# Causal attention of the second layer: nine-fold bf16 stacks in one bank each, against plain fp32 on four 32-row tiles of the array

## The chip, the cores and the metric

The kernel runs on one core of one Trainium2 chip. The metric is the device time of one launch in microseconds (us). Three runs of the kernel before took 5902.98, 5903.97 and 5895.77 us, median 5902.98.

## The reference

The program is a two-layer model on x of shape (2, 2048, 128), in fp32. Only the attention of the second layer is touched by the change. Cut to it:

```
x = x + L1_attn(layernorm(x))            # then a mixture-of-experts layer
q, k, v = h @ Wq, h @ Wk, h @ Wv         # 16 heads of 8 columns each
scores  = q k^T / sqrt(8)                # causal: keys up to the query's own position
p       = softmax(scores)                # over up to 2048 keys
out     = (p v) @ Wo                     # per sequence of 2048, 2 sequences
```

Ahead of it stand a retention layer and six layers of windowed attention with feed-forward; behind it the experts. None of these changes.

## The kernel before

Engines are programmed by hand, each with its own instruction stream, and meet only by semaphores. The names below are those of the code.

**Work.** The attention is cut into 8 groups (NG), each of 4 heads (GH) of one sequence. A group is worked in two passes. The first pass finds the largest score of every query: for each of 16 blocks of 128 queries (qt) and each chunk of up to 512 keys (kc) PE multiplies, and DVE takes the maximum over the keys (first_max, line 818). The second pass works with scores turned round (keys on the partitions, 512 queries of a chunk c in the free dimension): an item (c, kt) is one block of 128 keys against one chunk of queries, and a group has 40 items (ITEM). PE makes the scores of 4 heads (second_scores, line 1206), with the negated maximum added through extra rows of the contraction, ACT takes the exponential (exps, line 612), and PE multiplies with the values (second_values, line 1219), whose ninth column of ones sums the probabilities. At the end of a chunk the result is copied, turned and divided by the sum (copy_o, turn_o, store_o).

**Precision.** PE multiplies bf16 here. Each q and each k is written as a sum of three bf16 parts (high, middle, low), and all nine products of parts are stacked on the contraction dimension: 9 x 8 = 72 rows (KR), 75 with the three parts of the maximum. The parts are made once for all heads after the projection (lines 1174 to 1177 on PE, 596 to 601 on ACT, 804 and 808 on DVE), written to a buffer in DRAM (line 347) and read back for each group as stacks (load_stacks, lines 355 and 359) into RA with TOK, or RB with XC. The causal mask on a diagonal block is one more bf16 product that is added (tri_q in line 1194, tri_k in line 1209). The values are multiplied in plain fp32, the four heads in four column tiles of the array (9 columns each at 0, 32, 64, 96).

**Order.** att_step(g) does the first pass of group g between the items of the second pass of group g - 1. Per item PE runs: scores of heads 0 and 1 into the pair of banks D01, scores of heads 2 and 3 into D67, half of the item's four first-pass products (one head each, in turn into the two banks of D23), the values of the item before, the other half. So there are nine steps: a first one with the first pass alone, seven mixed ones (the middle six in a hardware loop), and a last one with the second pass alone. A step begins when the stacks of its group have arrived (stacks_in0, stacks_in1); they are loaded into the buffers that the group two before has left, after its last product. At the end of a step DVE combines the maxima, splits them in three parts (split_max), PE turns them, and SP copies them as rows into the stack (max_rows, line 367).

## Time and profile before

| | us |
|---|---|
| median of three runs | 5902.98 |
| the profiled execution | 5908.11 |
| its span, first to last instruction | 5906.1 |
| second-layer attention within the span, from its first projection (3911.5) to the first product of its output projection (5268.5) | 1357 |

| engine | busy us | share of the span |
|---|---|---|
| PE matmul | 5179.1 | 88% |
| PE weight load | 3133.2 | 53% |
| DVE | 3948.9 | 67% |
| ACT | 2684.4 | 45% |
| POOL | 2643.7 | 45% |

The mean granted clock of TensorE is 0.916 of full speed. Shares over the whole span say little here, since the attention in question is 23% of it and has its own pace. Matmuls are pipelined, and the duration of one in the trace holds the time in which its results drain; how close two of them follow each other is read from their starts. An fp32 matmul stands in the trace as two records, each with its own weight load.

### The profile page before, as it was taken

The page shows a single profiled execution, that of the slowest core. Times are in us where ns is not written, and L with a number is a line of the kernel's source. Part 1 is how long each engine was busy: PE and PEld are TensorE (multiplying, and loading weights), DVE is VectorE, ACT ScalarE, POOL GpSimd, SP SyncE. Part 2 cuts the span into 40 slices and gives each one's busy share as a digit, 9 for nine tenths or more (in the row PEclk, how much of TensorE's full clock was granted, in tenths as well). Part 3 has the DMA queues.
Part 4 walks back from the last instruction along what each step waited for, and adds up shares of the span by engine and source line. Part 5 has one row for each costly group of instructions (what it writes and reads, how often), then busy time and mean ns, then how long its engine had stood idle before and what let it go on. Part 6 is the DMA issues. An engine that isn't in the chain of part 4 may idle for free.

```text
span 5906.1 us, 163733 instructions
## 1 busy us (share of the span) xinstructions
PE 5179.1 (88%) x71504; PEld 3133.2 (53%) x71696; DVE 3948.9 (67%) x5079; ACT 2684.4 (45%) x3457; POOL 2643.7 (45%) x947
## 2 busy tenths in 40 slices
PE   8899889988998899989998899867777887798999
PEld 5566556664666466646665566532222222246776
DVE  5988488956986588748983889437566666623333
ACT  1565445644665365535653556421444444451111
POOL 2888378845885488628881788310000000000000
PEclk7999899989999899989998999875888888888999
DMA  1111101110111011101111111020111000100000
GB/s 51 31 37 37 46 27 37 39 53 19 39 37 60 12 38 37 39 34 35 37 39 40 31 37 39 20 62 14 17 18 17 12 12 12 17 33 2 4 4 5
DMA packets 94224, 173.85 MB, mean 29 GB/s; under 512 B 23641, under 2 KB 35554, under 8 KB 91874
## 3 DMA queue, kind: packets, MB, share of 16 engines
q1 hardware_dynamic: 93538, 163.67, 10.6%
q8 instruction: 557, 9.13, 0.7%
q14 instruction: 129, 1.06, 0.1%
HBM read 55.71 MB, written 8.39 MB: 11 GB/s over the span
## 4 chain that ended last, share of the span: by engine, by line
PE 76%; DVE 8%; issue 5%; ACT 4%; DMA 3%; POOL 2%; SPq 1%; DVEq 0%; ACTq 0%; POOLq 0%
PE D L1127 7%; PE D L1046 6%; PE D L1061 5%; PE D L1068 5%; PE D L1191 4%; PE D L978 4%; PE D L1219 4%; PE D L1310 4%; PE D L1085 4%; PE D L1026 3%; PE D L1206 3%; PE D L1094 3%; PE D L1096 3%; PE D L1034 3%; DVE mxp L818 3%
## 5 line engine op out<-in xcount | busy, mean ns | idle before, releaser
L423 POOL TENSOR_TENSOR rn<-ss,mhalf 128x32 f32<-128x32 f32 x192 | 1212.2, 6313 | 314.3 <-DVE ss L711 312.2
L818 DVE TENSOR_REDUCE mxp<-D 128x1 f32<-128x512 f32 (+3 forms) x1280 | 722.2, 606 | 417.6 <-PE D L1194 268.9
L612 ACT ACTIVATE hh<-D 128x1024 f32<-128x1024 f32 (+1 forms) x320 | 283.8, 936 | 605.5 <-PE D L1209 477.0
L1127 PE MATMUL D<-PTb,V 64*64 64x32 f32 x24576 | 415.7, 222 | 60.2 <-issue 42.8
L769 DVE TENSOR_TENSOR TOK<-D,RA 128x1024 f32<-128x1024 f32 x384 | 466.4, 1215 | 0.0
L428 POOL TENSOR_TENSOR hh<-hh,rr 128x1024 f32<-128x1024 f32 x192 | 364.6, 1899 | 219.8 <-DVE rr L739 219.5
L432 POOL TENSOR_TENSOR XC<-XC,TOK 128x1024 f32<-128x1024 f32 x132 | 311.5, 2360 | 335.2 <-DVE TOK L769 335.0
L1127 PEld LDWEIGHTS D<-PTb,V 64*64 64x64 f32 x24576 | 396.7, 138 | 102.5 <-issue 102.1
L709 DVE TENSOR_REDUCE ss<-TOK 128x32 f32<-128x2048 f32 x192 | 436.9, 2276 | 1.1 <-POOL rn L423 1.1
L558 ACT ACTIVATE V<-D 128x512 f32<-128x512 f32 x384 | 229.3, 597 | 451.5 <-PE D L1094 384.7
L263 POOL TENSOR_TENSOR rstd<-var_s,mhalf 128x4 f32<-128x4 f32 x96 | 96.3, 1007 | 717.2 <-DVE var_s L238 717.2
L1046 PE MATMUL D<-OTb,RB 128*128 128x128 f32 x3072 | 396.5, 285 | 14.7 <-ACT OTb L515 13.6
L1061 PE MATMUL D<-RB,XN 128*128 128x512 f32 x768 | 372.9, 609 | 40.3 <-DVE TOK L769 39.4
L1046 PEld LDWEIGHTS D<-OTb,RB 128*128 128x128 f32 x3072 | 378.9, 201 | 17.6 <-ACT OTb L515 15.1
L765 DVE TENSOR_TENSOR XC<-D,RA 128x1024 f32<-128x1024 f32 x264 | 321.6, 1218 | 90.2 <-ACT TOK L547 82.8
L1068 PE MATMUL D<-RB,XN 128*128 128x512 f32 x768 | 365.5, 599 | 2.6 <-DVE TOK L769 2.4
L515 ACT ACTIVATE OTb<-D 128x1024 f32<-128x1024 f32 x192 | 196.9, 1025 | 321.8 <-PE D L1127 321.8
L547 ACT ACTIVATE TOK<-D 128x1024 f32<-128x1024 f32 x192 | 196.4, 1023 | 304.1 <-PE D L1061 218.8
L612 ACT ACTIVATE V<-D 128x1024 f32<-128x1024 f32 (+2 forms) x320 | 256.3, 851 | 166.9 <-PE D L1206 88.0
L434 POOL TENSOR_TENSOR XC<-XC,TOK 128x1024 f32<-128x1024 f32 x132 | 311.6, 2361 | 0.0
L1085 PEld LDWEIGHTS D<-kTb,qTb 64*32 64x32 f32 x24576 | 254.0, 105 | 89.0 <-issue 89.0
L1191 PE MATMUL D<-TOK,RA 72*128 72x512 bf16 (+3 forms) x640 | 229.9, 407 | 80.1 <-DMA TOK<-parts_dram 44.9
(219 smaller groups left out, 10307.2 us busy)
## 6 DMA issues: line engine op xcount, KB each, us to landing
V<-V SPq DMA_DIRECT2D x936, 64.0 KB, 2.0
V<-V SPq DMA_DIRECT2D x192, 192.0 KB, 2.4
RA<-tabs_dram SPq DMA_DIRECT2D x6, 2048.0 KB, 7.8
RB<-watt_dram SPq DMA_DIRECT2D x6, 2048.0 KB, 12.2
parts_dram<-hh SPq DMA_DIRECT2D x48, 128.0 KB, 2.3
RA<-parts_dram SPq DMA_DIRECT2D x12, 384.0 KB
TOK<-parts_dram SPq DMA_DIRECT2D x36, 128.0 KB
RB<-parts_dram SPq DMA_DIRECT2D x12, 384.0 KB
```

The lines of the kernel that those rows point to most:

```text
L423: pool.tensor_tensor(rn[:, st % 2, :], ss[:, :], mhalf[:, :], ALU.pow).then_inc(s["powed"], 1)
L428: pool.tensor_tensor(sh, sh, rr[:, :].unsqueeze(2).to_broadcast([P, HEADS, 64]), ALU.mult).then_inc(s["pnorm"], 1)
L612: act.activation(PTE[n % 2][:, 2 * half:2 * half + 2, 0:CH - r * P], ST2[half][:, :, 0:CH - r * P], ACT.Exp, scale=float(HD) ** -0.5)\
L709: dve.tensor_reduce(ss[:, :], SQH.rearrange("p (a d) -> p a d", d=DH), AX.X, ALU.add).then_inc(s["reduced"], 1)
L769: return dve.tensor_tensor(swapped.rearrange("p (a q d) -> p a q d", q=2, d=32), src[:, :].rearrange("p (a q d) -> p a q d", q=2, d=32)[:, ...
L818: dve.tensor_reduce(mxp[:, h, qt, kc:kc + 1], PB[2 + n % 2][:, 0:first_pass_keys(qt, kc)], AX.X, ALU.max).then_inc(s["max1"], 1)
L1046: m = pe.matmul(D23[:, 0:P], WO[:, p, :], OTb[:, n % 2, p * P:(p + 1) * P], start=(p == 0), stop=(p == PAIRS - 1))
L1061: m = pe.matmul(PB[x], xb, WQ[:, x * CH:(x + 1) * CH], start=True, stop=True)
L1068: m = pe.matmul(PB[2 + x], xb, WK[:, x * CH:(x + 1) * CH], start=True, stop=True)
L1085: m = pe.matmul(D45[32 * r:32 * r + 32, at:at + 64], qTb[hs, p * P + 32 * r:p * P + 32 * r + 32], KT[n % 2][hs, p, 32 * r:32 * r + 64], st ...
L1127: m = pe.matmul(D01[64 * h:64 * h + 64, at:at + WIN], VW[n % 2][ks, (0 if r % 2 else 2) + h, p * DH:(p + 1) * DH], PTb[ks, p * P + 32 * r: ...
L1191: m = pe.matmul(bank[:, 0:keys], QST[p][0:KR, h * SEQ + qt * P:h * SEQ + (qt + 1) * P], KST[p][0:KR, h * SEQ + kc * CH:h * SEQ + kc * CH + ...
```

## The change

The stacks in bf16 and their way through DRAM go. The projection of q and k (project_group, line 1150 of the changed kernel) is made per group in fp32 with weights that are laid out so that each of the 4 heads has its 8 rows at the start of its own 32 partitions (wqk); one full product gives one chunk of q or k, 8 per group, and ACT copies it to SBUF (copy_qk). In the k copy a bias of one fills the ninth row of every head, and SP writes the negated maxima into the ninth row of q (max_rows), so that a second-pass product contracts 9 rows and a first-pass product 8. The four heads sit in four 32-row tiles of the array. A product of one head is one fp32 matmul of 128 stationary columns.

The work is cut into units of two heads (hp = 0 or 1): S units (second-pass scores) and F units (first pass). A unit takes one of three pairs of banks, D01, D23 and D67, in turn (pair_of), and waits for the reader of the unit three places ahead of it (released_by). One flat sequence of 320 items replaces the steps: at place `at` PE runs S0 and S1 of item at - 20 (LAG), F0 and F1 of first-pass item `at`, and the values of item at - 21. ACT takes the exponential of a unit at a time, DVE the maxima of two heads in one instruction. The mask of the first pass is still the added tri_q; that of the second pass is now a POOL instruction on the probabilities (cut_diagonal). Maxima are combined, turned and written per chunk, not per group. DVE's copy of the result goes to ACT (copy_o). Everything is written out, with no hardware loop.

```diff
+        WQK = OTb[:, 0, :].rearrange("p (a g n) -> p a g n", a=2, g=4)
+        QK = [[r[:, 0:SEQ], r[:, SEQ:2 * SEQ]] for r in (RA[:, :], RB[:, :], XS)]
...
+        PTE = [hh[:, 0:4, :], V2[:, :, :], V3[:, :, :]]
...
+        PAIR = [D01, D23, D67]
...
-        FIRST = [(h, qt, kc) for h in range(GH) for qt in range(NT) for kc in range(qt // 4 + 1)]
-        NF = len(FIRST) // ITEMS
-        assert NF * ITEMS == len(FIRST)
+        FIRST = [(qt, kc) for qt in range(NT) for kc in range(qt // 4 + 1)]
+        assert len(FIRST) == ITEMS
+        TOTAL = NG * ITEMS
+        LAG = 20
+        ENDS = [4, 12, 24, 40]
...
+        def units_at(at):
+            return [(kind, at, hp) for kind, hp in (("S", 0), ("S", 1), ("F", 0), ("F", 1))
+                    if (at >= LAG if kind == "S" else at < TOTAL)]
+        UNITS = [u for at in range(TOTAL + LAG) for u in units_at(at)]
+        UNIT_NO = {u: m for m, u in enumerate(UNITS)}
+        def pair_of(unit):
+            return PAIR[UNIT_NO[unit] % 3]
+        def released_by(unit):
+            m = UNIT_NO[unit] - 3
+            if m < 0:
+                return None, 0
+            kind, at, hp = UNITS[m]
+            return ("exp2", 2 * (at - LAG) + hp + 1) if kind == "S" else ("max1", 2 * at + 1 + hp)
...
+        def proj_at(at):
+            g, n = divmod(at, ITEMS)
+            x, rest = divmod(n - 4, 4)
+            return (g + 1, x // 2, x % 2) if g + 1 < NG and rest == 0 and 0 <= x < 8 else None
...
+            def max_rows(cg):
+                g, c = divmod(cg, CB)
+                sp.wait_ge(s["neg_copied"], cg + 1)
+                for h in range(GH):
+                    sp.dma_start(QK[g % 3][0][32 * h + HD:32 * h + HD + 1, c * CH:(c + 1) * CH].rearrange("r (x n) -> r x n", n=P),
+                                 nT[4 * h:4 * h + 4, cg % 2, :]).then_inc(s[f"neg_rows{cg % 2}"], 16)
...
+                pool.affine_select(out=PTE[i % 3][:, :, 0:P], in_=PTE[i % 3][:, :, 0:P], compare_op=ALU.is_ge, fill=0.0, base=0,
+                                   pattern=[[0, GH], [1, P]], channel_multiplier=-1).then_inc(s["diag_cut"], 1)
...
+            def copy_qk(g, c, qk):
+                act.wait_ge(s["qk_proj"], g * 8 + 2 * c + qk + 1)
+                dst = QK[g % 3][qk][:, c * CH:(c + 1) * CH]
+                if qk == 0:
+                    act.activation(dst, PB[5], ACT.Copy).then_inc(s["qk_copied"], 1)
+                else:
+                    act.activation(dst, PB[5], ACT.Identity, bias=ones_row).then_inc(s["qk_copied"], 1)
+            def exps(i):
+                g, n = divmod(i, ITEMS)
+                c, kt = ITEM[n]
+                r = max(0, kt - 4 * c)
+                if i >= 3:
+                    act.wait_ge(s["pv2"], i - 2)
+                for hp in range(2):
+                    act.wait_ge(s["score2"], 2 * i + hp + 1)
+                    act.activation(PTE[i % 3][:, 2 * hp:2 * hp + 2, 0:CH - r * P],
+                                   pair_of(("S", i + LAG, hp))[:, :].rearrange("p (h n) -> p h n", h=2)[:, :, 0:CH - r * P],
+                                   ACT.Exp, scale=float(HD) ** -0.5).then_inc(s["exp2"], 1)
...
-                dve.tensor_reduce(mxp[:, h, qt, kc:kc + 1], PB[2 + n % 2][:, 0:first_pass_keys(qt, kc)],
-                                  AX.X, ALU.max).then_inc(s["max1"], 1)
...
+                dve.tensor_reduce(mxp[:, 2 * hp:2 * hp + 2, qt, kc],
+                                  pair_of(("F", at, hp))[:, :].rearrange("p (h n) -> p h n", h=2)[:, :, 0:keys], AX.X, ALU.max)\
+                   .then_inc(s["max1"], 1)
...
+            def project_group(g, c, qk):
+                hg, b = divmod(g, 2)
+                if misc["qk_copied"]:
+                    misc_free()
+                pe.matmul(PB[5], WQK[:, qk, hg, :], chunk(XC, b * CB + c), start=True, stop=True).then_inc(s["qk_proj"], 1)
+                misc["qk_copied"] += 1
+            def first_pass(at, hp):
+                g, n = divmod(at, ITEMS)
+                qt, kc = FIRST[n]
                 keys = first_pass_keys(qt, kc)
-                if not (isinstance(g, int) and g == 0 and n < 2):
-                    pe.wait_ge(s["max1"], g * len(FIRST) + n - 1)
                 diag = kc == qt // 4
-                bank = PB[2 + n % 2]
-                m = pe.matmul(bank[:, 0:keys], QST[p][0:KR, h * SEQ + qt * P:h * SEQ + (qt + 1) * P],
-                              KST[p][0:KR, h * SEQ + kc * CH:h * SEQ + kc * CH + keys], start=True, stop=not diag)
+                if hp == 0 and qt % 4 == 0 and kc == 0:
+                    pe.wait_ge(s["qk_copied"], 8 * g + 2 * (qt // 4) + 2)
+                sem_name, count = released_by(("F", at, hp))
+                if count:
+                    pe.wait_ge(s[sem_name], count)
+                banks = pair_of(("F", at, hp))
+                for x in range(2):
+                    rows = slice(32 * (2 * hp + x), 32 * (2 * hp + x) + HD)
+                    m = pe.matmul(banks[:, x * CH:x * CH + keys], QK[g % 3][0][rows, qt * P:(qt + 1) * P],
+                                  QK[g % 3][1][rows, kc * CH:kc * CH + keys], start=True, stop=not diag)
                 if diag:
-                    m = pe.matmul(bank[:, keys - P:keys], ident_b[:, :], tri_q[:, :], start=False, stop=True)
+                    for x in range(2):
+                        m = pe.matmul(banks[:, x * CH + keys - P:x * CH + keys], ident_b[:, :], tri_q[:, :], start=False, stop=True)
                 m.then_inc(s["score1"], 1)
-            def second_scores(g, p, n):
+            def second_scores(i, hp):
+                g, n = divmod(i, ITEMS)
                 c, kt = ITEM[n]
                 r = max(0, kt - 4 * c)
-                for half in range(2):
-                    it = g * ITEMS + n
-                    pe.wait_ge(s["exp2"], 2 * it + half + 1)
-                    for x in range(2):
-                        h = 2 * half + x
-                        q0 = h * SEQ + c * CH + r * P
-                        m = pe.matmul(ST2[half][:, x, 0:CH - r * P], KST[p][0:KR + 3, h * SEQ + kt * P:h * SEQ + (kt + 1) * P],
-                                      QST[p][0:KR + 3, q0:q0 + CH - r * P], start=True, stop=kt < 4 * c)
-                        if kt >= 4 * c:
-                            m = pe.matmul(ST2[half][:, x, 0:P], ident_b[:, :], tri_k[:, :], start=False, stop=True)
-                    m.then_inc(s["score2"], 1)
...
+                pe.wait_ge(s["exp2"], 2 * i + 2)
+                if kt >= 4 * c:
+                    pe.wait_ge(s["diag_cut"], diagonals(i))
...
+            def turn_max(cg):
+                misc_free()
+                pe.wait_ge(s["max_all"], cg + 1)
+                pe.transpose(PB[5][0:GH * CB, 0:P], mxa[:, :, :].rearrange("p h x -> p (h x)"), ident).then_inc(s["neg_turned"], 1)
+                misc["neg_copied"] += 1
...
-                for n in range(ITEMS):
-                    if g2:
-                        second_scores(g - 1, p2, n)
-                    if g1:
-                        for x in range(NF // 2):
-                            first_pass(g, p1, n * NF + x)
...
+            for at in range(TOTAL + LAG + 4):
+                i = at - LAG
+                if 0 <= i < TOTAL:
+                    second_scores(i, 0)
+                    second_scores(i, 1)
+                if at < TOTAL:
+                    first_pass(at, 0)
+                    first_pass(at, 1)
+                if 1 <= i <= TOTAL:
+                    second_values(i - 1)
+                if chunk_end(at - 2) is not None:
+                    turn_max(chunk_end(at - 2))
+                if chunk_end(i - 3) is not None:
+                    turn_o(chunk_end(i - 3))
+                if proj_at(at) is not None:
+                    project_group(*proj_at(at))
...
+    wqk = np.zeros((128, 2, 4, 4, 32), np.float32)
+    for x, n in enumerate("qk"):
+        wqk[:, x, :, :, 0:8] = a["L1_attn_W" + n].T.reshape(128, 4, 4, 8)
+    d["wqk"] = wqk.reshape(128, 2, 4, 128)
```

PE, one full item in a step of before: S units of an item are L1206 (D01, D67), first-pass products L1191 (D23), the mask L1194, values L1219.

```order
L1206 MATMUL D01<-RA,TOK 128x512 [waits exp2]
L1206 MATMUL D01<-RA,TOK 128x512
L1202 REGISTER_ALU
L1206 MATMUL D67<-RA,TOK 128x512 [waits exp2]
L1206 MATMUL D67<-RA,TOK 128x512
L1188 REGISTER_ALU
L1191 MATMUL D23<-XC,RB 128x512 [waits max1]
L1188 REGISTER_ALU
L1191 MATMUL D23<-XC,RB 128x512 [waits max1]
L1219 MATMUL D45<-V2,qTb 9x512 [waits exp2]
L1219 MATMUL D45<-V2,qTb 9x512 x3
```

PE, the same place in the changed kernel: L1187 are the S units, L1167 the F units, L1171 the mask, L1204 the values; this is one full item and the scores of the next.

```order
L1187 MATMUL D01<-RA 128x512 [waits exp2]
L1187 MATMUL D01<-RA 128x512
L1187 MATMUL D23<-RA 128x512 [waits max1]
L1187 MATMUL D23<-RA 128x512
L1167 MATMUL D67<-RB 128x512 [waits max1]
L1167 MATMUL D67<-RB 128x512
L1167 MATMUL D01<-RB 128x512 [waits exp2]
L1167 MATMUL D01<-RB 128x512
L1204 MATMUL D45<-V2,qTb 9x512 [waits exp2]
L1204 MATMUL D45<-V2,qTb 9x512 x3
```

Where S had D01 and D67 to itself and F the two banks of D23, all three pairs now go round: the second F unit takes over the pair D01 from the first S unit of the same item, and stands ahead of the values.

PE, an item of the changed kernel whose F units lie on the diagonal, and at which a chunk's maxima are turned (L1212):

```order
L1167 MATMUL D01<-RB 128x256 [waits max1]
L1167 MATMUL D01<-RB 128x256
L1171 MATMUL D01<-tri_q,ident_b 128x128 x2
L1167 MATMUL D23<-RB 128x256 [waits exp2]
L1167 MATMUL D23<-RB 128x256
L1171 MATMUL D23<-tri_q,ident_b 128x128 x2
L1204 MATMUL D45<-V3,qTb 9x512 [waits diag_cut,exp2]
L1204 MATMUL D45<-V3,qTb 9x512 x3
L1212 MATMUL D45<-con,mxa 16x128 [waits o_stored,max_all,neg_copied,qk_copied]
```

The mask product follows each F unit, between products in row tiles, and the values wait for POOL's cut too. Chunk work that stood at the end of a step now stands between items.

## Rows read from the trace of the kernel before

**Rows 1.** Busy time by stretch: start:end, length, then each engine, PEclk, DMA share, GB/s

```profile
3911.00:3988.00 77.00, 25.41 (x100) 15.57 (x100) 21.52 (x35) 22.47 (x41) 16.05 (x12) 0.68 0.57 121
3988.00:4104.00 116.00, 87.42 (x227) 19.93 (x226) 93.10 (x172) 0.00 (x0) 0.00 (x0) 0.50 0.10 16
4104.00:4231.00 127.00, 118.00 (x785) 42.84 (x783) 97.42 (x196) 67.53 (x80) 1.00 (x4) 0.96 0.00 1
4231.00:4262.00 31.00, 0.00 (x0) 0.00 (x0) 0.00 (x0) 0.00 (x0) 0.00 (x0) 0.50 0.54 78
5179.00:5269.00 90.00, 82.07 (x570) 23.27 (x571) 5.73 (x24) 68.42 (x82) 0.00 (x0) 0.93 0.04 9
```

**Rows 2.** One line each: duration ns min/median/max, first and last start

```profile
L1174 PE MATMUL D<-XC,wC x16: 592/595/1219, 3911.5 to 3940.3; 128*128 128x512 f32 x16
L966 PE MATMUL D<-TOK,wC x16: 592/594/697, 5268.5 to 5277.7; 128*128 128x512 f32 x16
```

**Rows 3.** SP's queue in order of time: start, us, engine, line, count

```profile
4099.63 1.79 SPq L367 DMA_DIRECT2D RA<-nT  x3
...
4231.00 1.75 SPq L367 DMA_DIRECT2D RB<-nT  x3
...
4233.57 1.03 SPq L359 DMA_DIRECT2D TOK<-parts_dram  x3
...
5178.67 1.75 SPq L367 DMA_DIRECT2D RB<-nT  x3
```

**Rows 4.** Timeline of two full items within a mixed step

```profile
4347.55 1.94 ACT L612 ACTIVATE V<-D 128x1024 f32<-128x1024 f32 x2 [1.67 <-PE D L1206]
...
4350.36 1.94 ACT L612 ACTIVATE hh<-D 128x1024 f32<-128x1024 f32 x2 [0.87 <-PE D L1206]
```

**Rows 5.** Narrow windows of the timeline at one item's values, last step

```profile
5256.11 0.38 PE L1206 MATMUL D<-RB,XC 75*128 75x512 bf16 x1
...
5256.42 0.62 PE L1219 MATMUL D<-hh,PTb 128*9 128x512 f32 x4
...
5256.85 0.61 PE L1219 MATMUL D<-hh,PTb 128*9 128x512 f32 x4
5257.39 0.10 PEld L1206 LDWEIGHTS D<-RB,XC 75*128 75x128 bf16 x1 [0.86 <-ACT V L612]
```

**Rows 6.** Timeline, last step: what releases PE and what releases ACT

```profile
5253.89 1.94 ACT L612 ACTIVATE hh<-D 128x1024 f32<-128x1024 f32 x2 [0.26 <-PE D L1206]
...
5255.88 0.11 PEld L1206 LDWEIGHTS D<-RB,XC 75*128 75x128 bf16 x2 [0.57 <-ACT hh L612]
...
5257.90 0.22 PE L1209 MATMUL D<-tri_k,ident_b 128*128 128x128 bf16 x1
...
5258.16 1.02 ACT L612 ACTIVATE hh<-D 128x1024 f32<-128x1024 f32 x1 [0.38 <-PE D L1209]
```

**Rows 7.** Timeline of fp32 products in the layers ahead: full array, then tiles

```profile
3004.73 0.33 PE L1026 MATMUL D<-con,SQ 128*128 128x128 f32 x1
...
3004.73 1.09 PE L1026 MATMUL D<-con,SQ 128*128 128x128 f32 x8
...
3000.68 1.94 PE L1127 MATMUL D<-PTb,V 64*64 64x32 f32 x116
...
3012.28 0.26 PE L1085 MATMUL D<-kTb,qTb 64*32 64x64 f32 x4
```

**Rows 8.** Groups by line and form: busy us, mean ns, idle before

```profile
L612 ACT ACTIVATE hh<-D 128x1024 f32<-128x1024 f32 x256 | 248.8, 1021 | 556.7 <-PE D L1209 428.2 <-PE D L1206 128.4
L612 ACT ACTIVATE hh<-D 128x512 f32<-128x512 f32 x64 | 34.9, 595 | 48.8 <-PE D L1209 48.8
...
L755 DVE TENSOR_REDUCE mx<-D 128x16 f32<-128x1024 f32 x192 | 232.8, 1212 | 6.9 <-PE D L1085 6.5
```

**Rows 9.** One line: duration ns min/median/max, start

```profile
L446 POOL TENSOR_SCALAR_AFFINE_SELECT tri_q<-tri_q x1: 292/292/292, 3910.0 to 3910.0; 128x128 bf16<-128x128 bf16 x1
```

**Rows 10.** The page's DMA issues: count, KB each, us to landing

```profile
parts_dram<-hh SPq DMA_DIRECT2D x48, 128.0 KB, 2.3
```

More of the change, by code:

```diff
@@ L382, in _ @@
+            for cg in range(CHUNKS):
+                max_rows(cg)
+            sp.wait_ge(s["pv2"], TOTAL)
             sp.dma_start(EW1, t["ew1"].rearrange("e p n -> p e n")).then_inc(s["moew_in"], 16)
@@ L591, in _, with copy_o @@
+            def copy_o(cg):
+                g, c = divmod(cg, CB)
+                act.wait_ge(s["pv2"], g * ITEMS + ENDS[c])
+                if cg >= 1:
+                    act.wait_ge(s["o_turned"], cg)
+                act.activation(oTs, PB[4], ACT.Copy).then_inc(s["o_copied"], 1)
+            for c in range(CB):
+                for qk in range(2):
+                    copy_qk(0, c, qk)
             for c in range(NC):
                 act.wait_ge(s["c_proj"], c + 1)
-                if c >= 2:
-                    act.wait_ge(s[f"split_out{c % 2}"], 96 * (c // 2))
@@ L897, in _ @@
+            for at in range(TOTAL + LAG + 4):
+                if at < TOTAL:
+                    first_max(at, 0)
+                    first_max(at, 1)
+                if chunk_end(at) is not None:
+                    chunk_max(chunk_end(at))
+                if chunk_end(at - 2) is not None:
+                    negate_max(chunk_end(at - 2))
+                if chunk_end(at - LAG - 3) is not None:
+                    store_o(chunk_end(at - LAG - 3))
             for c in range(NC):
@@ L1212, in second_values @@
-            def second_values(g, p, n):
+                if hp == 0 and kt == 0:
+                    cg = g * CB + c
+                    pe.wait_ge(s[f"neg_rows{cg % 2}"], 64 * (cg // 2 + 1))
+                sem_name, count = released_by(("S", i + LAG, hp))
+                pe.wait_ge(s[sem_name], count)
+                banks = pair_of(("S", i + LAG, hp))
+                for x in range(2):
+                    rows = slice(32 * (2 * hp + x), 32 * (2 * hp + x) + HD + 1)
+                    m = pe.matmul(banks[:, x * CH:x * CH + CH - r * P], QK[g % 3][1][rows, kt * P:(kt + 1) * P],
+                                  QK[g % 3][0][rows, c * CH + r * P:(c + 1) * CH], start=True, stop=True)
@@ new lines, in _ @@
+            for c in range(NC):
+                if c >= 2:
+                    pe.wait_ge(s["c_vcopy"], c - 1)
+                for b in range(NBLK):
+                    m = pe.matmul(PB[6 + c % 2][:, b * P:(b + 1) * P], XC[:, c * CH + b * P:c * CH + (b + 1) * P], wC[:, 0, :],
+                                  start=True, stop=True)
+                m.then_inc(s["c_proj"], 1)
+            pe.wait_ge(s["tri_ready"], 2)
+            pe.wait_ge(s["o_zero"], 1)
+            pe.wait_ge(s["c_vcopy"], NC)
```

349 lines of the change are left out of this document (103 added, 246 removed).

## The prediction

> **What bounds the kernel now.** I read the busy time by stretch first. Within the span the attention runs from its first projection at 3911.5 us to the first output projection at 5268.5 us [rows 2], 1357 us, and only this part changes. The stretches [rows 1] show four phases. For 77 us bf16 parts are made, stored and loaded again (PE busy 25 us). Then 116 us of first pass alone, at PEclk 0.50. Mixed steps of 127 us follow at 0.96, with PE busy for 118 and DVE for 97; between two of them stand 31 us with no engine at work, while DMA is at 0.54. A last stretch of 90 us has no first pass. SP's queue tells why the 31 us are there: the maxima's rows of a group leave at 4231.00, and the next stacks are asked for only behind them, from 4233 on [rows 3]. From 4099.6 to 5178.7 there are 7 steps, 154 us each on average.
>
> Within a step the timeline has ACT begin two full items at 4347.55 and 4350.36, 2.81 us apart, with ACT idle for 0.87 of them [rows 4]. PE fills this: four bf16 score products, four first-pass products and the values. ACT's pair takes 1.94 us, so PE's order of work is the pace, and DVE is second.
>
> **What goes.** The parts, their way through DRAM and 7 x 31 = 217 us of empty array between steps; also about 10 us at half clock behind each of these (a step has 0.96). A product of scores drops from 72 or 75 rows of bf16 to 8 or 9 of fp32. An fp32 product of 512 columns makes two records 0.43 us apart [rows 5], so it streams for 0.853 us, four times a bf16 one; if four row tiles work at once, the four heads cost 0.853 us as before. So the multiplying itself gains nothing, and the question is how items follow each other.
>
> **Do tiles overlap?** The values are four products in four column tiles; four first records stand at 5256.42 and four second ones at 5256.85 [rows 5], so all four run at once. For row tiles the nearest rows are tiles of 64 rows: 116 records of 64x64 tiles lie in 1.94 us, at most 17 ns each [rows 7], so a set of eight takes at most 0.134 us, while two loads of 64 columns in one tile need 0.109 (a 128-column load has a pitch of (1.09 - 0.33)/7 = 0.109 us). Four such tiles, two up and two across, work nearly together. The set is at most 0.025 us longer than one tile alone, at most 0.05 for loads of 128 columns. I take full overlap, with 0.03 us per unit for loads that meet. The bounds: 0, and 0.21 if the loads of the two heads queue (two loads of 0.109 ahead of the second head).
>
> **The new chain.** In the order S0, S1, F0, F1, values, with three pairs of banks, unit m waits for the reader of unit m - 3. F1 of an item thus waits until ACT has read S0 of the same item, and the values stand behind F1 on PE. The next S0 stands behind the values. With w for the us that a product streams (0.853 for 512 columns):
> - S0 from start to ACT: load 0.057 (a first record of 128 columns takes 0.33, of which it streams for 0.107 and drains for 0.165, [rows 7]), w, drain 0.165 (0.592 of L966 less 0.427, [rows 2]), release 0.04 (the mask ends at 5258.12, ACT starts at 5258.16, [rows 6]).
> - ACT: 0.595 for 512 and 1.021 for 1024 elements [rows 8], so w + 0.167; PE starts 0.05 behind its end (5253.89 + 1.94 = 5255.83, load at 5255.88, [rows 6]).
> - F1: 0.057 + w, no drain in the way.
> - Values: 0.01 + w, and a change of tiles on either side: 0.10 before (the bf16 product streams until 5256.11 + 0.21 = 5256.32, next load 5256.42) and 0.10 behind (stream ends 5257.28, load 5257.39) [rows 5].
>
> A full item: 4 x 0.853 + 0.262 + 0.167 + 0.05 + 0.057 + 0.01 + 0.19 = 4.15 us, against 2.81 now. In this time ACT works for 1.94 and DVE for 2 x 1.21 (128x1024 maxima, L755, [rows 8]); neither is the bound, and PE itself stands idle only from F0's end (1.8) to F1's start (2.2).
>
> A group has 17408 columns a head in 40 items, 85% of full, so 4 w are 2.90. Fixed parts 0.74, loads that meet 0.06. In 16 of 40 items F lies on the diagonal: the two mask products need the whole array, 0.26 us on F1 and some 0.05 a mean item where F0's mask delays F1 (narrow S beside a wide F). That is 0.16 a mean item. Sum 3.85 us, or 154 a group.
>
> **Work between items.** Eight projections a group, each 0.853 + 0.057 + one more change of tiles 0.10 = 1.01. They write a bank of their own and ACT's copy (0.6) lies beside the next S0. 52 of them: 52 us. Turning the maxima, 32 x 0.25, and the result, 32 x 0.59 (four at the pitch of 0.109 and a change): 27 us, of which the second was there before. POOL's cut of 512 elements is at most 4 x 0.29 = 1.2 us [rows 9] and has 3 us until the values ask for it: nothing; without this cover it would be 16 x 1.2 a group. The rows of maxima need four issues at 0.6 (three took 1.79, [rows 3]) and, like the parts, 2.3 us to land [rows 10]; with the turning and the negation some 5.2 us, and the tightest chunk has two items, 6.6 us: nothing, but close.
>
> **Ends.** Before the sequence: 8 projections, each followed by its copy since they share a bank, 1.75 us at full clock and more at half, and the values' projection: 27 us. Then 20 places with F alone. There DVE is the pace, 2.4 us for the two maxima of a full item [rows 8]; these places have 79% of the full columns, so 38 us, and 50 with masks, first latency and four projections at half clock. At the end 20 items without F, 2.0 each: 40 us, and 5 to the output projection. When S joins, some 8 us pass at the half clock.
>
> Sum: 27 + 50 + 300 x 3.85 + 52 + 27 + 40 + 5 + 8 = 1364 us, against 1357. The profiled execution took 5908.11, of which 5906.1 is span; 7 more is 5915, and the median of the runs lies 5 lower than that execution: 5910 us. Within 0.2%, about 12 us, a measurement cannot tell it from no change, so what the 217 us of empty steps give back the longer items take.
>
> **The rivals.**
> (B) Row tiles overlap only in part. For it: no row of the trace has tiles of 32 rows by 128 columns. Against: the 17 ns [rows 7]. The price: loads that queue, 0.21 on S and 0.21 on F1 in place of 0.06, 0.36 x 300 = 108, and up to 0.2 w more for the streams; 5990 to 6090, say 6030. It is decided on PE between the first and last record of four score products. The Trainium skill (TensorE: Matmul & The Clock Gate, Part 3, Measured speedup) states 3.07 times for four row tiles at N=512. By it a set would take 1.30 streams, 0.22 more on S and as much on F1, 0.44 x 300 = 130 us; no run here shows it yet.
> (C) The clock falls. For it: the first pass alone ran at 0.50 for 116 us with PE 75% busy in the records [rows 1], and the array is now idle or half filled in part of each item. Against: the last step, with its own waits, keeps 0.93. At 1.2 GHz three of the four streams double (ACT's stays): 3 x 0.725 and the masks, +2.3 us an item; half of the 300 items so cost 340 us, 6250, all of them 6600.
> (D) Row tiles run one after another: eight streams an item, +3 us, about 6800. The four records in one window of 0.04 us of L1085, in 64-row tiles, [rows 7] speak against it.
> (E) Faster: changes of tiles and loads hide (loads run ahead of products wherever no wait stands before them), 0.19 + 0.11 off each item: 300 x 0.30 = 90, 5820. Against: each change of tiles in rows 5 costs its 0.10.
>
> **How the numbers follow.** The forecast, chain and overlap as worked out, has 48%; its own range is 5870 to 5955, since 0.13 us an item is 40 us, and it falls 18 faster, 10 within 0.2%, 20 slower. B 20%, C 15%, D 4%, E 13%. That makes 31% faster, 10% the same, 59% slower. The range 5835 to 6270 holds the forecast, B and half of C, and leaves out D, the upper half of C and half of E, together under 20%.
>
> **What would show it.** Right, if full items in the middle follow at 4.1 to 4.2 us on ACT, with ACT idle for 2.2 of them; if L1167's second unit starts 0.05 us behind the end of the first exponential of its item, and L1204 right behind it; if four first records of L1187 stand within 0.1 us; if no stretch of 30 us without work is left; if PEclk is 1.0 in the mixed part. B shows in the starts of L1187's records, C in PEclk. Wrong in another way: if PE mostly waits for max1, DVE is in the chain, and I have left it out; if it waits for neg_rows or diag_cut, a cover named above was too thin.

## The result and the profile after

| | us |
|---|---|
| median after, 4 runs | 6738.0 (6723.49 to 6742.88) |
| median before, 4 runs beside them | 5899.38 (5891.22 to 5903.97) |
| ratio, 95% interval | 1.1419 [1.1396, 1.1442] |
| profiled span after | 6721.8 |
| granted clock over the span | 0.805, before 0.916 |

The change costs 839 us. The forecast was 5910, the range 5835 to 6270: wrong in sign and in size.

First the place. The output projection's first product, and the group projections (duration ns, then first and last start):

```profile
L932 PE MATMUL D<-TOK,wC x16: 592/595/1219, 6084.1 to 6094.6; 128*128 128x512 f32 x16
L1150 PE MATMUL D<-XC,OTb x128: 637/1114/1223, 3892.0 to 5709.5; 128*128 128x512 f32 x128
```

From 3892.0 to 6084.1 are 2192 us, against 1357 in [rows 2], 835 more. (This execution reached the attention 19.5 us earlier than the one before, 3892.0 against 3911.5, so the two spans differ by 816; behind the attention both take 638.) The whole loss lies in the attention. A projection product here has a median of 1114 ns; those of the output projection, the same shape, have 595. Something slows TensorE in this stage and lets go of it behind it. The profile's clock line (40 slices, tenths of full speed) and the stretches, with the columns of [rows 1], say what:

```profile
PEclk8999899899989998998999855555555555557999
```

```profile
3911.00:3945.00 34.00, 32.23 (x156) 17.57 (x155) 12.25 (x16) 6.66 (x11) 1.32 (x6) 0.65 0.00 1
3945.00:4000.00 55.00, 54.99 (x184) 19.09 (x182) 31.24 (x33) 8.23 (x11) 2.21 (x6) 0.50 0.00 0
4000.00:4100.00 100.00, 99.57 (x377) 29.54 (x379) 33.85 (x36) 26.50 (x34) 3.81 (x6) 0.50 0.00 1
5000.00:5100.00 100.00, 98.60 (x401) 29.18 (x397) 33.35 (x34) 27.01 (x35) 6.02 (x12) 0.55 0.00 1
6000.00:6050.00 50.00, 50.00 (x209) 11.80 (x205) 10.31 (x10) 18.02 (x22) 2.54 (x4) 0.50 0.00 1
```

Read them against [rows 1]. The 31 us without work are gone, and so is the DMA (share 0.54, now 0.00). But where a mixed step was granted 0.96, the stage now gets 0.50 to 0.55 from 3945 to 6050: nearly always the lower of the two levels, 1.2 GHz. It does so with PE at work for 98.60 of 100 us, so PE is not short of work. The Trainium skill (TensorE: Matmul & The Clock Gate, Part 1) lets the clock fall when the engine has been idle; these rows do not agree with that as the cause.

Now one full item. ACT's exponentials, four items in a row, then one item on all engines, then a narrow window (5007.095 to 5007.14) at its first products (timeline: start, us, engine, line; x is the count of records):

```profile
4912.02 1.94 ACT L608 ACTIVATE V<-D 128x1024 f32<-128x1024 f32 x2 [5.41 <-PE D L1187]
4919.12 1.94 ACT L608 ACTIVATE V<-D 128x1024 f32<-128x1024 f32 x2 [5.16 <-PE D L1187]
4926.21 1.94 ACT L608 ACTIVATE hh<-D 128x1024 f32<-128x1024 f32 x2 [5.16 <-PE D L1187]
4933.30 1.94 ACT L608 ACTIVATE V<-D 128x1024 f32<-128x1024 f32 x2 [5.16 <-PE D L1187]
```

```profile
5007.10 2.09 PE L1187 MATMUL D<-RA 9*128 9x512 f32 x8
5008.12 0.34 PEld L1167 LDWEIGHTS D<-RB 8*128 8x128 f32 x2 [0.50 <-issue]
...
5009.29 1.94 ACT L608 ACTIVATE hh<-D 128x1024 f32<-128x1024 f32 x2 [4.49 <-PE D L1187]
5010.36 0.50 PEld L1167 LDWEIGHTS D<-RB 8*128 8x128 f32 x4 [1.05 <-ACT hh L608]
...
5012.37 1.90 PE L1204 MATMUL D<-V,PTb 128*9 128x512 f32 x8
...
5014.20 0.52 PEld L1187 LDWEIGHTS D<-RA 9*128 9x128 f32 x8 [1.70 <-issue]
```

```profile
5007.10 0.30 PEld L1187 LDWEIGHTS D<-RA 9*128 9x128 f32 x4 [1.70 <-issue]
5007.10 1.24 PE L1187 MATMUL D<-RA 9*128 9x512 f32 x4
```

and the same line in this item, with the durations of its eight records (ns min/median/max; an fp32 product has two records, so four heads have eight):

```profile
L1187 PE MATMUL D<-RA x8: 1056/1136/1218, 5007.1 to 5008.1; 9*128 9x512 f32 x8
```

Three things stand here. The four first records together last 1.24 us, and the longest one of the eight 1.218: they start within 0.02 us, so the row tiles do run together. All eight records of four heads span 2.09 us with their drain. One after another four heads would stream for 4 x 2 x 0.853 = 6.8 us at this clock; here they take less than a third of it. By the 3.07 times that the Trainium skill states for four row tiles (TensorE: Matmul & The Clock Gate, Part 3, Measured speedup), and that the prediction cited under rival B, they would take an estimated 2.2 us before any drain, so this trace has more overlap than that.

The order of events is the predicted chain: S, first exponential, F1 0.05 behind its end (5009.29 + 1.02 = 5010.31, load at 5010.36), values, next S. And every leg on PE (the time from one event of the chain to the next) has about twice its forecast length: S to ACT 2.19, F1 to values 2.01, values to the next S 1.83; with ACT's 1.07 the item is 7.10, and ACT's rows stand 7.09 to 7.10 apart. The forecast was 4.15.

### The profile page after: what moved, and what is told of

Read it like the earlier page. It is cut to its first block, busy times and chain, and to the rows that moved or that the text cites. A ratio compares the mean times of both kernels' runs of the same rounds, so it can differ in the third digit from the quotient of the medians.

```text
span 6721.8 us, 164570 instructions
## 1 busy us (share of the span) xinstructions
PE 6315.2 (94%) x73664; PEld 3422.5 (51%) x73856; DVE 3857.7 (57%) x4247; ACT 2723.0 (41%) x3521; POOL 2710.1 (40%) x1071
## 4 chain that ended last, share of the span: by engine, by line
PE 86%; DVE 4%; ACT 4%; issue 3%; POOL 2%; DMA 0%; DVEq 0%; SPq 0%; ACTq 0%; POOLq 0%
PE D L1167 13%; PE D L1187 8%; PE D L1204 7%; PE D L1093 6%; PE D L1012 5%; PE D L1027 4%; PE D L1034 4%; PE D L944 4%; PE D L1294 4%; PE D L1051 3%; PE D L992 3%; PE D L1060 3%; PE D L1000 3%; PE D L1062 3%; PE D L1125 2%
## 5 line engine op out<-in xcount | busy, mean ns | idle before, releaser
L820 DVE TENSOR_REDUCE mxp<-D 128x2 f32<-128x1024 f32 (+3 forms) x640 | 677.8, 1065 | 1342.9 <-PE D L1167 812.0
L608 ACT ACTIVATE V<-D 128x1024 f32<-128x1024 f32 (+3 forms) x426 | 359.1, 894 | 842.8 <-PE D L1187 841.9
L463 POOL TENSOR_SCALAR_AFFINE_SELECT V<-V 128x512 f32<-128x512 f32 x84 | 53.3, 634 | 1260.1 <-ACT V L608 1260.1
L429 POOL TENSOR_TENSOR XC<-XC,TOK 128x1024 f32<-128x1024 f32 x132 | 311.6, 2361 | 334.9 <-DVE TOK L781 334.7
L1167 PE MATMUL D<-RB 8*128 8x512 f32 (+2 forms) x960 | 359.9, 935 | 9.1 <-ACT V L608 8.0
L1167 PE MATMUL D<-RA 8*128 8x512 f32 (+2 forms) x960 | 354.8, 950 | 7.2 <-ACT V L608 4.0
L608 ACT ACTIVATE hh<-D 128x1024 f32<-128x1024 f32 (+1 forms) x214 | 179.3, 889 | 434.5 <-PE D L1187 434.3
L463 POOL TENSOR_SCALAR_AFFINE_SELECT hh<-hh 128x512 f32<-128x512 f32 x44 | 27.9, 634 | 808.2 <-ACT hh L608 808.2
```

Source lines behind the costliest of these rows:

```text
L608: act.activation(PTE[i % 3][:, 2 * hp:2 * hp + 2, 0:CH - r * P], pair_of(("S", i + LAG, hp))[:, :].rearrange("p (h n) -> p h n", h=2)[:, : ...
L820: dve.tensor_reduce(mxp[:, 2 * hp:2 * hp + 2, qt, kc], pair_of(("F", at, hp))[:, :].rearrange("p (h n) -> p h n", h=2)[:, :, 0:keys], AX.X ...
L1167: m = pe.matmul(banks[:, x * CH:x * CH + keys], QK[g % 3][0][rows, qt * P:(qt + 1) * P], QK[g % 3][1][rows, kc * CH:kc * CH + keys], start ...
```

## The experiments

Theory 1: the clock is granted low because few rows of the array take part in the products (8 or 9 of each 32). Theory 2: it is low because of waits and changes between units. S is a second-pass unit, F a first-pass unit, 0 and 1 are the pairs of heads (hp). The kernel before, run beside each of them, had medians from 5899.7 to 5907.1; where two runs lie close, their ratios compare them better than their medians. The clock is the mean over the whole span.

| run | what differs from the changed kernel | median us | ratio to before, 95% | granted clock |
|---|---|---|---|---|
| e1_rows32 | 32 rows in F and S | 5948.81 | 1.0080 [1.0063, 1.0097] | 0.948 |
| e10_rows24 | 24 rows | 5983.03 | 1.0125 [1.0094, 1.0155] | 0.939 |
| e6_rows16 | 16 rows | 6710.2 | 1.1358 [1.1327, 1.1388] | 0.811 |
| e8_first_pass_rows32 | 32 rows in F, 9 in S | 6641.7 | 1.1239 [1.1206, 1.1273] | 0.824 |
| e2_values_early | values between F0 and F1 | 6900.3 | 1.1692 [1.1669, 1.1715] | 0.789 |
| e3_alternating | order S0, F0, S1, F1 | 6892.75 | 1.1679 [1.1656, 1.1702] | 0.795 |
| e4_rows32_values_early | 32 rows, values between | 6048.49 | 1.0227 [1.0201, 1.0254] | 0.928 |
| e5_rows32_alternating | 32 rows, order S0, F0, S1, F1 | 5982.31 | 1.0128 [1.0108, 1.0149] | 0.948 |
| e7_rows32_no_mask1 | 32 rows, no first-pass mask | 5899.8 | 0.9982 [0.9970, 0.9994] | 0.949 |
| e12_crossed_no_mask1 | e7, units crossed | 5898.84 | 0.9996 [0.9984, 1.0008] | 0.948 |
| e9_before_few_rows | kernel before, 8 and 11 rows | 6686.83 | 1.1318 [1.1286, 1.1351] | 0.802 |
| e11_before_no_mask1 | kernel before, no first-pass mask | 5890.0 | 0.9974 [0.9960, 0.9987] | 0.917 |

**All 32 rows.**

```diff
-                    rows = slice(32 * (2 * hp + x), 32 * (2 * hp + x) + HD)
+                    rows = slice(32 * (2 * hp + x), 32 * (2 * hp + x) + 32)
...
-                    rows = slice(32 * (2 * hp + x), 32 * (2 * hp + x) + HD + 1)
+                    rows = slice(32 * (2 * hp + x), 32 * (2 * hp + x) + 32)
```

> Every product of scores, in both passes, contracts all 32 rows of its tile in place of 8 or 9; the added rows hold zeros, so order, streams, loads and results stay as in the changed kernel. Theory 1 (the clock falls because the products fill too few rows of the array): the granted clock is about 1.0 through the mixed part and the time falls to where the chain was forecast, 5880 to 5960 us. Theory 2 (the clock falls because PE has gaps in every item, while it waits for the first exponential and between changes of tiles): rows change nothing, clock 0.5 to 0.55, 6738 us within 0.3%.

Two slices, and 789 us come back (6738.0 to 5948.8). Number of instructions, columns, waits and order are those of the changed kernel, and the added rows add nothing: they are zeros on both sides, but for the ninth row of k in F, which holds ones against zeros in q. The profile's clock line and two stretches of this run, the second one long:

```profile
PEclk8999899989998999989998999879999999998999
```

```profile
5000.00:5100.00 100.00, 94.02 (x621) 30.30 (x621) 55.76 (x56) 43.01 (x56) 8.60 (x16) 1.00 0.00 1
...
3990.00:5200.00 1210.00, 1129.04 (x7528) 369.81 (x7522) 635.85 (x684) 522.29 (x648) 80.56 (x144) 1.00 0.00 1
```

The clock is 1.00 over 1210 us, and PE is busy for less of the time than it was at half clock (94.02 against 98.60 of 100). Theory 1 holds, at 5948.8 within its 5880 to 5960, and this run also shows what the kernel would have been on the forecast's assumption. The same four legs, at the full clock:

```profile
4916.94 1.94 ACT L608 ACTIVATE hh<-D 128x1024 f32<-128x1024 f32 x2 [2.41 <-PE D L1187]
...
4918.02 0.30 PEld L1167 LDWEIGHTS D<-TOK 32*128 32x128 f32 x4 [1.15 <-ACT hh L608]
...
4919.08 1.05 PE L1204 MATMUL D<-V,PTb 128*9 128x512 f32 x8
...
4920.05 0.31 PEld L1187 LDWEIGHTS D<-TOK 32*128 32x128 f32 x8 [0.86 <-issue]
4920.06 1.14 PE L1187 MATMUL D<-TOK 32*128 32x512 f32 x8
```

```profile
4921.29 1.94 ACT L608 ACTIVATE V<-D 128x1024 f32<-128x1024 f32 x2 [2.41 <-PE D L1187]
```

```profile
L1187 PE MATMUL D<-TOK x8: 587/640/692, 4920.1 to 4920.6; 32*128 32x512 f32 x8
```

From ACT to ACT 4.35 us: 1.08 + 1.06 + 0.98 + 1.23. The forecast had 1.07, 1.01, 0.96 and 1.115. Of S's records, in the last fence, the longest (a first one, behind its load) has 0.692 and the shortest 0.587, so 0.105 of load stands bare, not 0.057. The same 0.105 fits F1's leg (0.105 + 0.853 + 0.10 = 1.06). S's records end at 4921.20 (4920.06 + 1.14) and ACT starts at 4921.29, a release of 0.09 where the forecast had 0.04. Of the excess of 0.19, the load twice makes 0.10 and the release 0.05; 0.04 is spread over the rest.

**The dose.** In the same two slices, 16 and then 24 rows; and 32 rows in the first pass's slice alone.

> 16 of the 32 rows of each row tile take part (the added rows are zeros), in place of 8 or 9 in the changed kernel and 32 in e1_rows32. Instructions, streams and loads are the same. Theory 1 (the share of rows that take part decides the granted clock) expects a granted clock between the two, and a time between them: 6100 to 6500 us if the clock follows the rows smoothly; 5940 to 5960 or 6720 to 6750 if it has a step on one side of 16 rows. Theory 2 (the gaps between units decide, and e1_rows32 only filled something else) expects no order by rows at all.

> 24 of the 32 rows of each row tile take part (the added rows are zeros). e6_rows16 ran at 6710 us, e1_rows32 at 5949. Theory 1 expects a time between them; 6000 to 6500 us if the clock follows the rows, 5945 to 5960 or 6690 to 6720 if it has one step.

> 32 rows take part in the first pass's products alone; those of the second pass keep their 9 rows (the changed kernel has 8 and 9, e1_rows32 has 32 and 32). Theory 1 in the form that each stream counts by its own rows expects a time between the two, 5950 to 6500 us, with a granted clock between 0.80 and 0.95; in the form that it takes the whole item above some share, it expects either 5945 to 5960 (above it) or 6730 to 6745 (below it).

One hundred us of each, sixteen rows, then twenty-four (two stretches), then the first pass alone (two stretches):

```profile
5000.00:5100.00 100.00, 98.71 (x384) 28.87 (x382) 30.35 (x32) 28.31 (x34) 3.18 (x5) 0.53 0.00 1
```

```profile
4500.00:4600.00 100.00, 95.94 (x531) 30.92 (x531) 47.33 (x49) 36.75 (x50) 8.55 (x16) 0.81 0.00 1
5000.00:5100.00 100.00, 93.82 (x622) 30.51 (x624) 54.00 (x56) 42.55 (x56) 8.56 (x16) 1.00 0.00 1
```

```profile
4500.00:4600.00 100.00, 99.57 (x379) 30.19 (x375) 33.05 (x36) 26.07 (x34) 3.81 (x6) 0.50 0.00 1
5000.00:5100.00 100.00, 98.38 (x450) 31.00 (x447) 38.61 (x40) 28.81 (x40) 8.56 (x16) 0.62 0.00 1
```

It is no even slope: 16 rows give back 28 us of the 789, little more than the runs of one kernel differ by, and 24 rows give back 755. With 24 the clock is full in some stretches and not in others. Neither time lies in a range that was expected: 6710.2 stands 10 us under the step's 6720 to 6750, and 5983.0 between the step's 5945 to 5960 and the slope's 6000 to 6500. Filling F alone gives back 96 us, far less than half; with S at its 9 rows the clock stays low most of the time. The expectation for e8 in its first form (5950 to 6500) was missed by 142 us, though its clock of 0.824 lies in the 0.80 to 0.95, and so was the second, since a part does come back.

**The converse, in the kernel before.**

```diff
-                m = pe.matmul(bank[:, 0:keys], QST[p][0:KR, h * SEQ + qt * P:h * SEQ + (qt + 1) * P],
-                              KST[p][0:KR, h * SEQ + kc * CH:h * SEQ + kc * CH + keys], start=True, stop=not diag)
+                m = pe.matmul(bank[:, 0:keys], QST[p][64:KR, h * SEQ + qt * P:h * SEQ + (qt + 1) * P],
+                              KST[p][64:KR, h * SEQ + kc * CH:h * SEQ + kc * CH + keys], start=True, stop=not diag)
```

> The converse, in the kernel before: its score products contract rows 64 to 72 and 64 to 75 alone, 8 and 11 rows of bf16 in place of 72 and 75; so 64 rows of parts are left out of the scores. Columns, instructions and waits stay. Theory 1 expects that the granted clock of the mixed steps falls from 0.96 towards 0.5 and the time rises by several hundred us (mixed steps of 127 us have 118 us of PE, so up to 100 us more in each of 8 groups: 6300 to 6700 us). The rival, that the fall needs fp32 streams in row tiles and not few rows in themselves, expects 5890 to 5930 us.

(The second pass's rows, KR + 3, begin at 64 in the same way. The 64 rows left out hold parts of q and k, so this run's scores are wrong and only its time is of use.) Groups, 4700 to 4800 us (line, shapes, count | busy us, mean ns), and a long stretch of this run:

```profile
L1206 PE MATMUL D<-RA,TOK 11*128 11x512 bf16 x60 | 28.9, 623 | 0.0
L1191 PE MATMUL D<-XC,RB 8*128 8x512 bf16 x52 | 28.4, 617 | 0.0
```

```profile
3990.00:5200.00 1210.00, 1046.69 (x3531) 245.98 (x3531) 511.68 (x994) 290.22 (x337) 4.03 (x16) 0.50 0.07 10
```

The same loss, in bf16, without row tiles, with DMA between the steps: 780 us slower than its kernel before, clock 0.50 over 1210 us. Fewer rows in each score product, with columns, instructions and waits as they were, took the clock away. So fp32 scores, row tiles, the grouping and the new waits are not needed for the loss. The rows left out held data, so this run alone would not tell the number of rows from what is in them; e1_rows32 does, since it adds zeros.

**The gaps.** The values moved between F0 and F1, and the alternating order, at 8 and 9 rows.

```diff
                 if at < TOTAL:
                     first_pass(at, 0)
-                    first_pass(at, 1)
                 if 1 <= i <= TOTAL:
                     second_values(i - 1)
+                if at < TOTAL:
+                    first_pass(at, 1)
```

```diff
-                if 0 <= i < TOTAL:
-                    second_scores(i, 0)
-                    second_scores(i, 1)
-                if at < TOTAL:
-                    first_pass(at, 0)
-                    first_pass(at, 1)
+                for hp in range(2):
+                    if 0 <= i < TOTAL:
+                        second_scores(i, hp)
+                    if at < TOTAL:
+                        first_pass(at, hp)
```

(In the second, the list that numbers the units is changed alike.)

> The values of the item before stand between the two first-pass units, so PE has work while the first exponential runs. Theory 2 (gaps): the clock goes up for most of the mixed part, and with a full item of about 3.9 us the time is 5850 to 6100. Theory 1 (rows): the clock stays at 0.5 to 0.55; PE is then full in each item (S 1.87, F 1.7 + 1.87, values 1.7, changes of tiles 0.4: 7.5 us against 7.1 now), and the time is 6700 to 6880 us.

> Units alternate S0, F0, S1, F1 on PE and in the turn of the three pairs, in place of S0, S1, F0, F1. At either theory the chain is nearly the same, since F1 still takes over the pair of S0 and stands ahead of the values; F0 stands between S0 and S1, so that only two tiles work at the start of an item. Theory 1: clock 0.5 to 0.6, 6700 to 6900 us. Theory 2: the gap before F1 becomes smaller (S1 and F0 fill it), so the clock may rise in part of the stretch: 6100 to 6600 us.

The stretch from 5000 to 5100 us, first of e2_values_early, then of e3_alternating:

```profile
5000.00:5100.00 100.00, 99.69 (x382) 28.79 (x374) 28.39 (x34) 26.67 (x31) 2.54 (x4) 0.50 0.00 1
```

```profile
5000.00:5100.00 100.00, 100.00 (x356) 32.13 (x355) 26.99 (x32) 25.82 (x29) 2.54 (x4) 0.52 0.00 1
```

PE is at work for all or nearly all of the time, and the clock is as low as ever (0.50, 0.52). Both orders cost some 160 us more; e2_values_early lies 20 us above the 6700 to 6880 that theory 1 gave it. Theory 2 falls as the cause of this loss.

**The same two orders at 32 rows.**

> All 32 rows of each row tile take part (the added rows are zeros, as in e1_rows32), and the units of an item alternate again: S0, F0, S1, F1, with the values last. It asks what the grouping itself is worth at the full clock. Theory 1 (the granted clock falls because few rows of the array take part) expects a granted clock near that of e1_rows32 (0.95) and a time between 5900 and 6020 us: in this order S1 waits for nothing but its own bank, F1 waits for the reader of S0, and a chain counted as for the grouped order comes to about the same 4.35 us for a full item. At the half clock alternating had cost 155 us more than grouping; theory 3 (grouping is worth the same 155 us at either clock, since it keeps the two S units' products and their loads in a row) expects 6080 to 6120 us.

> All 32 rows take part as in e1_rows32, and the values of the item before stand between F0 and F1 instead of behind F1, so that PE does not idle while it waits for the first exponential. If the prediction's chain is the bound as it was told (the wait of F1 for the exponential of S0), filling that wait takes up to 0.4 us off a full item: 5830 to 5880 us. The rival is that three pairs of banks for four units bind in any order: F1 then ends later, DVE's maximum of it (1.21 us) holds F0 of the next item, and the chain F1, drain 0.165, maximum 1.21, F0, values comes to 4.4 us: 5950 to 6010 us.

Grouping against alternating is worth 34 us at the full clock (5982.3 - 5948.8) and 155 at the half clock (6892.8 - 6738.0). So that part of the change is a gain at either level, and not the loss. Putting the values early is 100 us slower, 6048.5 where even the rival had 5950 to 6010; the waits (us in total, times, longest, from 5000 to 5100) and a stretch, first of e1_rows32, then of e4_rows32_values_early:

```profile
PEld D L1167 <- DVE mxp L820: 3.0, 9, 0.8
```

```profile
PEld D L1167 <- DVE mxp L820: 13.7, 19, 1.3
```

```profile
4100.00:4200.00 100.00, 95.95 (x569) 30.43 (x566) 45.60 (x50) 39.30 (x50) 7.28 (x14) 0.88 0.00 1
```

The wait for DVE's maximum (3.0 to 13.7 us of the 100) takes in part the place of the one for the exponential (19.8 to 12.0), as the rival said; but the clock is also below full in part of the run (0.88 here), so how the 100 us divide between the two stays open. It also says that 32 rows alone do not secure the full clock: here the order took some of it away, and no run shows why.

**The mask products.** In the first pass they are left out, so the maximum is taken over the future keys of the diagonal block too, another shift of the same exponentials; once on e1_rows32, once on the kernel before.

```diff
-                if diag:
-                    for x in range(2):
-                        m = pe.matmul(banks[:, x * CH + keys - P:x * CH + keys], ident_b[:, :], tri_q[:, :], start=False, stop=True)
```

> As e1_rows32, and the mask products of the first pass are left out: the maximum of a row is then taken over the future keys of the diagonal block too, which is another shift of the same exponentials. In e1_rows32 the two mask products stood in 16 of 40 items at 0.26 us. If PE is the chain there (theory 1, the prediction's chain), they cost 300 x 0.4 x 0.26 = 31 us and some 10 more from F0's mask and the places with F alone: 5905 to 5925 us, against 5949 for e1_rows32. The rival, that ACT's and DVE's readers set the pace of the diagonal items and the masks lie beside them, expects 5940 to 5955 us.

> The kernel before without the mask products of its first pass, as e7_rows32_no_mask1 has it (5900 us, 50 below e1_rows32). It asks whether that gain belongs to the row tiles. The kernel before has 16 mask products of 128 columns in bf16 a head and group, 0.06 us each as a stream: 64 x 8 x 0.06 = 31 us if PE is its pace everywhere, 5870 to 5885 us. The rival, that the first pass's reader on DVE (one maximum a head) sets the pace of those products, expects 5895 to 5907 us.

49 us off with row tiles by the medians (24 to 44 expected), 58 by the ratios; 17 off the kernel before, between the 22 to 37 of the one theory and the up to 12 of the other. With row tiles the mask stands in the chain. From e1_rows32, F1, its mask and the values of one item:

```profile
5263.75 1.13 PE L1167 MATMUL D<-RB 32*128 32x512 f32 x4
...
5264.81 0.28 PE L1171 MATMUL D<-tri_q,ident_b 128*128 128x128 bf16 x2
...
5265.02 1.05 PE L1204 MATMUL D<-V,PTb 128*9 128x512 f32 x8
```

The values start 1.27 us behind F1 in place of the 1.06 above, so the mask costs 0.21; in 16 of 40 items of 300 that is 25 us, about half of the gain, and the rest is not placed. With the mask gone the kernel of row tiles is level with the kernel before (0.9982), and so is the kernel before without its mask (0.9974): the two intervals overlap. So the row tiles gain nothing here over an old kernel that is given the same saving.

**Crossed units.** S of heads 0, 1 with F of heads 2, 3, and then the other way round, on top of e7: in the alternating order above, F's rows and the place of its maximum take `1 - hp` for `hp`.

> Built on e7_rows32_no_mask1 (32 rows, no mask products in the first pass; 5899.8 us). The units of an item alternate, but crossed: S of heads 0 and 1 with F of heads 2 and 3, then S of heads 2 and 3 with F of heads 0 and 1, then the values. Neighbouring units stand in other row tiles and have other readers (ACT and DVE), so each pair of streams may overlap: three streams in an item in place of four, and the second exponential no longer waits behind the first. If streams on PE are the bound, an item loses up to 0.6 us: 5750 to 5850 us. If three pairs of banks for four units are (a unit holds its pair for 0.107 + 0.853 + 0.165 + 0.04 and its reader, 1.02 or 1.21, and one stream of the values with its changes stands between), the order changes little: F of heads 0 and 1 still waits for the exponential and the next F for the other one, 5885 to 5910 us. The alternating order of e5_rows32_alternating lost 33 us; if its loss came from the same cause, this one loses it too: 5920 to 5945 us.

```profile
4916.38 0.70 PE L1184 MATMUL D<-TOK 32*128 32x512 f32 x2
4916.39 0.19 PEld L1167 LDWEIGHTS D<-RA 32*128 32x128 f32 x2
4916.40 0.70 PE L1167 MATMUL D<-RA 32*128 32x512 f32 x2
...
4917.36 1.02 PE L1184 MATMUL D<-TOK 32*128 32x512 f32 x4
...
4917.62 1.94 ACT L608 ACTIVATE hh<-D 128x1024 f32<-128x1024 f32 x2 [1.98 <-PE D L1184]
4918.69 0.30 PEld L1167 LDWEIGHTS D<-RA 32*128 32x128 f32 x4 [1.14 <-ACT hh L608]
```

Here the first S (L1184) and the first F (L1167) start 0.02 us apart and stream together, and the median is that of e7 within a microsecond (ratios 0.9996 and 0.9982, whose intervals overlap). But this is the only pair that overlaps: the second S starts at 4917.36, when the two have streamed, and the second F waits for the exponential as before (4917.62 + 1.02 = 4918.64, load at 4918.69). PE runs four streams one behind another (S with F, S, F, values), as many as in e7 (S with S, F, F, values), so no stream was taken out of the sum, and the chain S, exponential, F, values is unchanged. That fits three pairs of banks for four units as what holds F1 at the full clock; no run had a fourth pair, since the eight banks are in use, so it is the best reading and not shown alone.

## Why the prediction was wrong

- **The step that failed** is the weighing of rival C, "The clock falls", at 15%, and with it the forecast's silent use of full-clock durations for every product of the new chain. The sentence against C, "the last step, with its own waits, keeps 0.93", was no evidence: its score products have 75 rows [rows 5]. The change itself took 72 and 75 rows down to 8 and 9, which the prediction names under "What goes" and prices in columns alone. The runs put this in its place: with 8 and 9 rows the clock is 0.53 over the stage and the time 6738.0; with 32 it is 1.00 from 3990 to 5200 and 5948.8. C's own reasons, an array "idle or half filled in part of each item", were not the cause either: e1_rows32 keeps the wait for the first exponential and the F units that fill two of the four tiles, and has the full clock. So C named the right event for reasons that the runs do not bear out.
- **C's price.** +2.3 us for a mean item and 6600 for all items. Measured: 6738, and between the first S and the end of the last F 2044 us (3983.7 to 6028.2) against 1273 in e1_rows32 (3993.2 to 5266.0), 2.57 a mean item. On a full item three streams of 0.853 would be 2.56, and the item grew by 2.94 over the forecast (7.09 for 4.15). "Three of the four streams double" was right, but load, release and change of tiles grew with them: S's leg rose by 1.07, F1's by 1.00, that of the values by 0.87, ACT's not at all.
- **Overlap of tiles, rival B and D.** As forecast, 0.02 us between four first records, and 0.105 of bare load where B had two loads in a row. B and D are refuted.
- **The chain.** Right in its order and its one bound: F1 0.05 us behind the first exponential in both clocks. At full clock 4.35 for 4.15; the forecast's 0.06 for loads that meet is part of the difference, and some 0.13 is not covered. The mis-sized terms are the load (0.057 and 0.03 for loads that meet, measured 0.105, twice) and the release to ACT (0.04, measured 0.09). The stage of e1_rows32 has 1406 us (3908.5 to 5314.4) for 1364: 85 for 77 up to the first S, 1273 for the 1242 of the mixed part with its work between items, 48 for 45 behind. So at full clock too the change would have been 0.8% slower.
- **A count in "What goes".** Seven empty stretches of 31 us, 217 us, are one too many. Stacks are loaded behind six of the seven mixed steps; behind the seventh the next product (L1206) stands at 5182.19, 4 us after the step's last one (5178.13). The six have 30 to 32 us each, 186 in all. The sum of the forecast does not use the figure.
- **Covers.** All held. POOL's cut, one line (duration ns, first and last start) and the values that wait for it:

```profile
L463 POOL TENSOR_SCALAR_AFFINE_SELECT V<-V x84: 634/634/635, 3994.8 to 6079.4; 128x512 f32<-128x512 f32 x84
```

```profile
L1204 PE MATMUL D<-V,PTb 128*9 128x512 f32 (+3 forms) x856 | 168.0, 875 | 1.0 <-POOL V L463 1.0
```

  634 ns, half of the bound of 1.2 us, and 1.0 us of waiting in the whole stage. The rows of maxima were waited for once, 0.8 us. At the full clock, where items are shorter, e1_rows32 has 1.0 us for the cut and 1.6 for the rows. DMA share 0.00: the 186 us of empty steps did go away.
- **Rival E** (loads and changes hide) is refuted: a change of tiles still costs 0.11 at full clock (4919.08 + 0.01 + 0.853 = 4919.94, next load 4920.05).

## What to carry to other kernels

Products that contract few rows can take the clock from a whole stage. Before packing small contractions into row tiles, count the rows that each product addresses, and where the profile's granted clock falls while PE is busy, fill the tile's remaining rows: zeros did it here, and no run shows a price for them. It is not the only condition: the kernel before had 0.50 in its first pass alone, with 72 rows and PE busy for 75% [rows 1], and e4_rows32_values_early lost part of the clock with 32. Read a clock level as evidence only for products with as many rows. Where the new order rests on waits for banks, price load, drain and change of tiles at both clock levels, since the level is what decides.

## What was not expected of the hardware

- PE at work for 98 to 99% of a stretch and the clock at 0.50 to 0.55, for over 2 ms; 32 rows in each tile, the added ones zeros, bring 1.00. Rows that are addressed count, even where they hold only zeros.
- It holds for bf16 products that are not tiled as well (8 and 11 rows, clock 0.50).
- With 24 rows of 32 the same program has stretches at 0.81 and at 1.00; from 3990 to 5200 us the mean is 0.97, and with 16 rows it is 0.54.
- Four fp32 row tiles of 32 x 128 stream together with 0.02 us between the first and the last start; their four loads leave 0.10 us bare in front.
- Taking out the mask products of the first pass is worth 49 us between row tiles and 17 in the old order.
